# Layer 3's mixture of experts: half of each tile's weighted sum moves from VectorE to ScalarE and GpSimd, and the bias product moves behind the first experts

## What is computed

```python
router_logits = einsum('bsd,ed->bse', x, W_router) + b_router
router_weights = softmax(router_logits)       # the two largest of 8 kept, the rest set to 0
expert_out = einsum('bsd,eod->bseo', x, W_experts) + b_experts
out = einsum('bseo,bse->bso', expert_out, router_weights)
...
x = x + tanh(g_ffn[3]) * L3_ffn(layernorm(x))
```

## Time and profile before

| | us |
|---|---|
| median of 3 runs | 1064.07 (1063.49 to 1065.72) |
| the profiled execution, its own time | 1065.34 |
| its span in the profile | 1063.6 |
| PE busy | 905.5 (85%) |
| DVE busy | 709.5 (67%) |
| ACT busy | 457.7 (43%) |
| POOL busy | 104.8 (10%) |

### The profile page before, as it was taken

One profiled execution on the slowest core, in us unless ns is written; L12 is line 12 of the kernel. 1 busy time (PEld: TensorE's weight loads), 2 busy tenths in 40 slices (PEclk: granted clock), 3 DMA queues, 4 the chain that ended last, 5 costly groups with the idle time before them and its releaser, 6 DMA issues.

```text
span 1063.6 us, 14472 instructions
## 1 busy us (share of the span) xinstructions
PE 905.5 (85%) x4795; PEld 608.3 (57%) x4795; DVE 709.5 (67%) x2190; ACT 457.7 (43%) x1101; POOL 104.8 (10%) x175
## 2 busy tenths in 40 slices
PE   2459899997877878978999999999999888889967
PEld 2434544543343555665667677677667666667744
DVE  0962652639295695895848858658856787877845
ACT  0514455567767656566354263253153222212200
POOL 3100000004031130130000101000100200000000
PEclk9669999998898999999999999999999999999987
DMA  9400000000000000000000000000000000000000
GB/s 260 144 2 1 1 1 1 1 1 1 0 1 1 1 1 1 1 2 1 1 1 2 1 1 1 1 1 1 1 1 1 1 1 11 1 11 1 1 11 10
DMA packets 12066, 12.72 MB, mean 12 GB/s; under 512 B 3759, under 2 KB 7897, under 8 KB 11993
## 3 DMA queue, kind: packets, MB, share of 16 engines
q10 hardware_dynamic: 5536, 8.04, 2.5%
q1 hardware_dynamic: 6072, 3.24, 1.1%
q0 software_dynamic: 384, 0.53, 0.3%
HBM read 10.75 MB, written 1.05 MB: 11 GB/s over the span
## 4 chain that ended last, share of the span: by engine, by line
PE 57%; DVE 23%; ACT 6%; issue 5%; POOL 2%; POOLq 0%; ACTq 0%; DVEq 0%
PE bank L1608 10%; PE bank L1596 6%; PE bank L1518 5%; PE bank L1598 5%; PE bank L1597 5%; PE bank L1533 4%; PE bank L1403 4%; DVE x L1313 3%; DVE nm L1153 3%; DVE hb L1297 3%; DVE hb L1288 2%; ACT PTs L957 2%; PE bank L1573 2%; DVE x L1277 2%; PE bank L1356 2%
## 5 line engine op out<-in xcount | busy, mean ns | idle before, releaser
L994 ACT ACTIVATE hb<-bank 96x512 f32<-96x512 f32 (+1 forms) x160 | 95.0, 594 | 244.8 <-PE bank L1598 244.1
L1608 PEld LDWEIGHTS bank<-m_w,hb 128*128 128x128 f32 (+1 forms) x1280 | 165.9, 194 | 22.5 <-issue 4.9
L1596 PE MATMUL bank<-parts,m_w_lo 128*96 128x512 f32 (+1 forms) x320 | 151.9, 475 | 29.9 <-DVE hb L1288 20.5
L1608 PE MATMUL bank<-m_w,hb 128*128 128x128 f32 (+1 forms) x1280 | 175.4, 281 | 2.2 <-DVE hb L1288 2.0
L1297 DVE SCALAR_TENSOR_TENSOR hb<-hb,bank 96x512 f32<-96x512 f32 (+1 forms) x160 | 109.0, 682 | 93.8 <-ACT hb L994 93.0
L1598 PE MATMUL bank<-parts,m_w_hi 128*96 128x512 f32 (+1 forms) x320 | 127.2, 398 | 0.0
L1597 PE MATMUL bank<-parts,m_w_hi 128*96 128x512 f32 (+1 forms) x320 | 127.0, 397 | 0.0
L1288 DVE TENSOR_TENSOR hb<-hb,bank 96x512 f32<-96x512 f32 (+1 forms) x160 | 109.7, 686 | 8.6 <-PE bank L1598 3.0
L1533 PE MATMUL bank<-Qs,KT 112*77 112x512 f32 x192 | 94.5, 517 | 10.9 <-ACT PTs L957 8.8
L1596 PEld LDWEIGHTS bank<-parts,m_w_lo 128*96 128x96 f32 (+1 forms) x320 | 59.0, 184 | 78.1 <-DVE hb L1288 32.6
L1029 DVE RECIPROCAL rden<-bank 128x16 f32<-128x16 f32 x48 | 12.2, 255 | 122.3 <-PE bank L1356 122.3
(11 more groups left out here) (271 smaller groups left out, 1525.9 us busy)
## 6 DMA issues: line engine op xcount, KB each, us to landing
m_w<-in_L_ffn_w_dram ACTq DMA_DIRECT2D x2, 1024.0 KB, 11.5
nat_m<-in_L_ffn_W_dram ACTq DMA_DIRECT2D x1, 1408.0 KB, 16.8
x<-in_x_dram SPq DMA_DIRECT2D x4, 256.0 KB, 8.4
out_dram<-x SPq DMA_DIRECT2D x4, 256.0 KB, 2.0
f_out<-in_L_ffn_Wout_dram POOLq DMA_DIRECT2D x8, 64.0 KB, 7.7
m_w<-in_L_ffn_W_experts_dram ACTq DMA_DIRECT2D x1, 512.0 KB, 17.2
ctxn<-in_ctx_dram SPq DMA_DIRECT2D x4, 38.5 KB
Wq<-in_L_xattn_Wq_dram SPq DMA_DIRECT2D x2, 64.0 KB
```

Source lines behind the costliest of these rows:

```text
L994: act.activation(hb[n % 3][0:m, :], bank[UP[u, n]][0:m, :], ACT.Tanh, scale=0.5).then_inc(*chunk_act.up(u, n))
L1596: pe.matmul(dst, w_lo, x_hi, start=True, stop=False)
L1608: op = pe.matmul(bank[7][:, t * P:(t + 1) * P], hb[n % 3][0:m, t * P:(t + 1) * P], wd, start=i == 0 and t == 0, stop=ends_expert(k, n) and ...
```

## The change

Of a tile's eight experts, DVE still weighs and sums the first four, in steps with e = 0, from bank 0. ScalarE weighs the other four (e = 4, from bank 1) into an SBUF buffer `weighed[t % 2]`, which reuses room of the attention's probabilities (`PTs`), with one `activation` Copy for each expert whose scale is the gate column. GpSimd adds the four weighed blocks in pairs, one add of 128 x 256 and one of 128 x 128. DVE adds the sum into x, one tile later (`rest`). PE's bias product and DVE's add of it move from before tile 0 into step n = 2, behind the first two products. F3's body has nine steps in place of eight, so the merge with F2 shifts a little. Bank 0 is now read by DVE alone and bank 1 by ACT alone.

```diff
+    weighed = [PTs[:, 1 + i, :].rearrange("p (j d) -> p j d", d=P) for i in range(2)]
-        return {... "F3": len(tiles)}.get(k) ...
+        return {... "F3": len(tiles) + 1}.get(k) ...
 # gpsimd body
+                for n in range(steps_body(kind(u))):
+                    if kind(u) == "F3" and n % 2:
+                        t = n // 2
+                        y = weighed[t % 2]
+                        pool.wait_ge(*rows_weighed.at(u, t))
+                        pool.tensor_tensor(y[:, 0:2, :], y[:, 0:2, :], y[:, 2:4, :], ALU.add).then_inc(*rows_paired.up(u, t))
+                        pool.wait_ge(*rows_paired.at(u, t))
+                        pool.tensor_tensor(y[:, 0, :], y[:, 0, :], y[:, 1, :], ALU.add).then_inc(*rows_summed.up(u, t))
 # scalar body
+                    act.wait_ge(*logits_vector.at(u, "whole"))
+                    if b:
+                        act.wait_ge(*x_done.at(("A", u[1] - 2)))
+                    for n, (t, e) in enumerate(tiles):
+                        if e:
+                            if t >= 2:
+                                act.wait_ge(*x_done.at(u, t - 2, "rest"))
+                            act.wait_ge(*chunk_psum.at(u, n))
+                            for j in range(E3):
+                                op = act.activation(weighed[t % 2][:, j, :], bank[n % 2][:, j * P:(j + 1) * P], ACT.Copy,
+                                                    scale=gw[s][:, t, e + j:e + j + 1])
+                            op.then_inc(*rows_weighed.up(u, t))
+                        yield
+                    yield
 # vector body
-                    (the wait for the bias and the add to x, before the first step)
+                    def rest(t):
+                        dve.wait_ge(*rows_summed.at(u, t))
+                        dve.wait_ge(*x_done.at(u, t, E3 - 1))
+                        dve.tensor_tensor(x[b][:, t, :], weighed[t % 2][:, 0, :], x[b][:, t, :], ALU.add) ...
                     for n, (t, e) in enumerate(tiles):
+                        if n == 2:
+                            (x_done of tile 0, the wait for the bias and the add to x)
+                        if e == 0:
                             (the wait for the product and its four operations)
+                            if t:
+                                rest(t - 1)
                         yield
+                    rest(T - 1)
+                    yield
 # tensor body
-                    (gates_ready, free(3), the bias product, before the first step)
                     for n, (t, e) in enumerate(tiles):
+                        if n == 2:
+                            (gates_ready, free(3), the bias product)
                         ...
-                        reader[d] = (x_done, u, t, e + E3 - 1)
+                        reader[d] = (rows_weighed, u, t) if e else (x_done, u, t, E3 - 1)
```

More of the change, by code:

```diff
@@ L658, in main @@
         "gates_ready").split())
+    rows_weighed, rows_paired, rows_summed = (sig(n) for n in "rows_weighed rows_paired rows_summed".split())
     (chunk_psum, chunk_act, chunk_silu, chunk_ready, ffn_psum,
@@ L704, in steps_body @@
             return H + 1
-        return {"A3": 3, "F0": 2 * (C0 + 1), "F3": len(tiles)}.get(k) or 3 * (len(chunks[k]) + LATE)
+        return {"A3": 3, "F0": 2 * (C0 + 1), "F3": len(tiles) + 1}.get(k) or 3 * (len(chunks[k]) + LATE)
     def steps_tail(k):
@@ L837, in body @@
             def body(u):
-                for _ in range(steps_body(kind(u))):
+                for n in range(steps_body(kind(u))):
[6 more added lines that the diff above has]
+                        pool.tensor_tensor(y[:, 0, :], y[:, 0, :], y[:, 1, :], ALU.add).then_inc(*rows_summed.up(u, t))
                     yield
@@ L999, in body @@
                 if k == "F3":
-                    for _ in tiles:
+                    act.wait_ge(*logits_vector.at(u, "whole"))
[10 more added lines that the diff above has]
+                            op.then_inc(*rows_weighed.up(u, t))
                         yield
+                    yield
             def tail(u):
@@ L1303, in body @@
                 if k == "F3":
[L1304 to L1307, removed]
-                    for n, (t, e) in enumerate(tiles):
[L1309 to L1315, removed]
+                    def rest(t):
+                        dve.wait_ge(*rows_summed.at(u, t))
+                        dve.wait_ge(*x_done.at(u, t, E3 - 1))
+                        dve.tensor_tensor(x[b][:, t, :], weighed[t % 2][:, 0, :], x[b][:, t, :], ALU.add) \
+                            .then_inc(*x_done.up(*((u,) if t + 1 == T else (u, t, "rest"))))
@@ new lines, in body @@
+                    for n, (t, e) in enumerate(tiles):
+                        if n == 2:
+                            dve.wait_ge(*x_done.at(u, 0, E3 - 1))
+                            dve.wait_ge(*ffn_psum.at(u, "bias"))
+                            dve.tensor_tensor(x[b][:].rearrange("p t d -> p (t d)"), bank[3][:],
+                                              x[b][:].rearrange("p t d -> p (t d)"), ALU.add).then_inc(*x_done.up(u, "bias"))
+                            dve.wait_ge(*x_done.at(u, "bias"))
+                        if e == 0:
+                            dve.wait_ge(*chunk_psum.at(u, n))
+                            for j in range(E3):
+                                if j:
+                                    dve.wait_ge(*x_done.at(u, t, j - 1))
+                                dve.scalar_tensor_tensor(out=x[b][:, t, :], in0=bank[n % 2][:, j * P:(j + 1) * P],
+                                                         scalar=gw[s][:, t, j:j + 1], in1=x[b][:, t, :],
+                                                         op0=ALU.mult, op1=ALU.add).then_inc(*x_done.up(u, t, j))
+                            if t:
+                                rest(t - 1)
@@ L1316, in body @@
                         yield
-                    x_done.counts[(u,)] = x_done.counts[(u, T - 1, MOE3 - 1)]
+                    rest(T - 1)
+                    yield
             def tail(u):
@@ L1641, in body @@
                 if k == "F3":
[L1642 to L1647, removed]
                     pe.wait_ge(*xf_low.at(u))
                     for n, (t, e) in enumerate(tiles):
+                        if n == 2:
+                            pe.wait_ge(*gates_ready.at(u))
+                            free(3)
+                            for i in range(T):
+                                op = pe.matmul(bank[3][:, i * P:(i + 1) * P], gT[:, i * P:(i + 1) * P], m3_b[:], start=i == 0, stop=i == T - 1)
+                            op.then_inc(*ffn_psum.up(u, "bias"))
+                            reader[3] = (x_done, u, "bias")
                         d = n % 2
```

## The result

The changed kernel takes 1056.95 us (median of 4 executions, 1055.78 to 1060.12) beside 1063.78 for the kernel before on the same chip (1062.61 to 1065.72, 4 executions): a ratio of 0.9941, 95% interval 0.9914 to 0.9968, or 6.8 us less. The forecast was 1055.7 in a range of 1052.0 to 1060.5. The profiled execution took 1060.12 with a span of 1058.4, so it is 3 us above its own median, and part of the story is why. Two executions of the kernel before that stand beside its second trace ran in a slower state (1219 and 2284 us) and are left out of every number.

The account below looks back on a forecast made before the run. DVE was taken to bound F3's bodies in streams 0 to 2, and its own chain stream 3. Savings of 6.1 us (streams 0 to 2) and 2.3 (stream 3) made 8.4, giving 1055.7 us, range 1052 to 1060.5.

Parts of the forecast that it names:

- Streams 0 to 2: F3's bodies beside F2: PE becomes the bound at 94% busy, saving 2.7, 1.6 and 1.8 us, together 6.1.
- the bias product's move: F3's start: bias product (1.15 us) falls behind product 1; its DVE add (0.69) is moved, not removed.
- the ninth step: F3's merge with F2: the extra step shifts F2 by less than a step, costed at nothing, 1 us either way.
- Stream 3: Running alone at the end: store at 1058.6 against 1061.17, 2.6 us saved, taken as 2.3 (1.3 to 2.8).
- ACT: Weighing an odd product: four weighed blocks take 1.14 us, bounds 0.95 and 1.45.
- POOL: Adding the weighed blocks in pairs: 0.61 and 0.40 us, 1.08 a tile with hand-over, bounds 0.9 and 1.35.
- `rest(t - 1)`: DVE's add of the earlier tile's sum, merged part: its 2.3 us path is hidden for t = 0 to 2.
- A: F3 of streams 0 to 2: PE takes over as the bound, 7 to 11 us won; chance 0.62.
- B: F3's hand-overs: waits at `rest(3)`, for bank 0 or late F2 pairs eat half, 3 to 5 us won; chance 0.18.
- C: POOL's adds: DVE waits at every `rest`; gain gone at 2.3 us a pair, 1072 us at 2.8; chance 0.05.
- D: A3 after F3 starts earlier: more than 11 us won, 1 to 1.5 for streams 0 and 1 each; chance 0.10.
- E: F2's own chain holds PE, only stream 3 counts and the step shift cancels it: 1063 to 1065 us; chance 0.05.

Follow-up runs that it names:

- second trace: The kernel before run once more with no edit: 1064.57 us, ratio 1.0008 to itself.
- the two series of the changed kernel: The changed kernel measured first, 1056.95 us (ratio 0.9941), and again with no edit, 1058.67 us (ratio 0.9949).
- relieved kernel: Changed kernel in eight steps, with DVE doing one of its four weighed sums per tile in streams 0 to 2: 1054.01 us, ratio 0.9917.
- eight steps: The changed kernel without the ninth step, `rest(3)` standing at the end of the eighth: 1058.07 us, ratio 0.9947.
- the two others with nine steps: Changed kernel with ACT and POOL taking experts 0 to 3, DVE 4 to 7 in two banks: 1057.10 us; changed kernel with one more POOL add per tile: 1060.68.
- four eight-step ones: Changed kernel in eight steps: as such, 1058.07 us; streams 0 to 2 only, 1059.43; DVE's products in two banks, 1056.27; ACT and POOL taking experts 0 to 3, 1056.41.
- streams 0 to 2 alone: Streams 0 to 2 as changed but in eight steps, stream 3 as in the kernel before: 1059.43 us, ratio 0.9951.
- the pair at 2.09: The changed kernel with a further POOL add of 128 x 256 into an unused buffer ahead of each pair: 1060.68 us, ratio 0.9974.

## Why the prediction was right, point by point

**In short:** the mechanism was right, the time fell into the range, and the sum was too large: 8.4 us forecast, 6.8 and 5.5 in the two series of the changed kernel. That the total came as near as it did is in part luck, since an oversized term and a missing one have opposite signs.

**The bound and the direction** were right. DVE was the bound of F3's bodies, and with half of its sums gone PE is: 94% and 91% busy, windows of 16.36 and 16.60 us. The relieved kernel confirms it from the other side, with 2 to 3 us for another 13.7 of DVE's work.

**Streams 0 to 2** were forecast at 6.1 us and gave 4.5 in nine steps (5.1 to 6.0 in eight) at full clock. They are not spread as forecast: streams 0 and 1 were to win 4.3 and the stretch beside them won 5.3 to 5.8; stream 2 was to win 1.8 and its stretch lost about 1 in nine steps and won 0.1 in eight. Three terms of the sum are to be mended. First, stream 2's window was cut to the last operation on x, 1.3 us past PE's last down product, and that end counted as PE's idle time. A window of the kernel before that ends with PE's last down product:

```profile
988.00:1013.40 25.40, 23.57 (x136) 19.18 (x134) 22.37 (x55) 4.16 (x7) 0.00 (x0) 1.00 0.00 1
```

PE was busy 93% already. From the forecast's own start, 991.57, to PE's end at 1013.36 it is 20.00 of 21.79 us, 92%, and lifting that to 94% is worth 0.5, not 1.8. Second, the bias product's move was costed at nothing in these streams, and alone it wins about 1.9 us of F. Third, the ninth step costs 1 us. So mended the sum says 6.1 - 1.3 + 1.9 - 1.0 = 5.7, still 1.2 more than was measured: the relief of DVE won less than the 94% promised, or part of it is what the move had won already. No kernel here has the relief without the move, so the share of each isn't shown.

**The clock** was no term at all in streams 0 to 2. The changed kernel's traces lost 5.1 and 1.7 us to it in F, the two others with nine steps 2.0 and 3.5, the kernel before's two 0.2 and 3.4. Some low stretches come back at the same place in kernels with the same steps (near 857 to 863 in all four nine-step traces, between 933 and 939 in four eight-step ones), others don't, and not every wait of PE is followed by one. Whether the change makes them more frequent is not settled: two traces of the kernel before are too few.

**Stream 3** was walked right: 2.6 from the walk, 2.62 measured, a tile 2.57 for 2.65. Some 0.2 of it is the clock's: in "streams 0 to 2 alone", whose stream 3 is that of before, the stretch takes 15.04 at a granted clock of 1.00, where the trace before took 15.26 at 0.89; at full clock the change is worth 2.4. The cut to 2.3 for a product at low clock was unneeded: the granted clock was 1.00 in that window.

**ACT** 1.14 for four blocks, exactly (the overlap that the forecast gives as 105 ns works out at 109 from its rows). **POOL** 1.29 from the start of the first add to `rest` (1054.34 to 1055.63) where 1.08 + 0.04 was taken, inside the bound of 1.35. The row behind the price, L834 in the earlier trace rows, is a multiplication that reads one operand twice, and not an add; the adds here read two. **`rest(t - 1)`** never waits for t = 0 to 2 (2.5 us of waiting in all, in two places, 1.56 of them at the end), and the wait at `rest(3)` was 0.95 in stream 0 and none in streams 1 and 2, where up to 1 was forecast. In eight steps it is 1.15, 1.43 and 1.83.

**The rivals.** A's mechanism happened, but its gain stayed below its 7 to 11 us with 5.5 to 6.8; of its range, 1053 to 1057.5, the first series (1056.95) is inside and the second (1058.67) isn't. B gave 3 to 5, which the intervals of the two series (3.4 to 9.1 and 3.8 to 6.9 us) don't exclude. Its mechanism isn't seen in the changed kernel, where DVE stands 0.95 for `rest(3)` in one of streams 0 to 2 and not 2.3 in each; in eight steps it comes nearer, and still F is shorter there. C did not happen, since POOL's pair took 1.29 with its hand-over, under the 1.8 from which C counts. Its price was not far off: with the pair at 2.09 its rule gives 16 x 0.29 = 4.6 us of loss, and 2.7 to 3.5 were measured. D needed the following A3 to start earlier; even the relieved kernel, with 8 us in F, only reached 9 in all by its ratio. E is refuted by the kernel with streams 0 to 2 alone, which won 5 us without stream 3. The page cited with rival C, the Trainium skill's "SBUF — State Buffer", § Who interferes with whom, has the pair right: `rest`, with two SBUF inputs, slowed beside POOL's adds, and the weighed sums, with one input in PSUM, did not (0.35 either way). But `rest` took 0.17 us more where the add still ran on for 0.30 (1046.06 to 1046.36), and 0.42 more with 0.62 beside adds, so a block in full isn't what these rows show; and in the changed kernel `rest` came when POOL was done.

## What to carry to other kernels

When work is moved off an engine, look for what else moved with it, and run that part alone: here a small product and its add, moved behind the first products, let DVE's first sum start 0.7 to 1.35 us sooner and alone won about 1.9 us in the merged streams, where the whole change won 4.5. Look at the stretches one by one as well: all of the 4.5 and more came beside one feed-forward, and beside the other the kernel lost about 1. Cut a window at the end of the engine that is to become the bound, not at the end of the one being relieved. And set low-clock time aside before comparing two traces: here it differed by 3 us between two executions of one kernel, as much as the effect in question.

## What the runs showed of the hardware that was not expected

- A GpSimd add of two different f32 operands in SBUF took 461 ns for 128 columns and 730 for 256, 2.1 ns a column, where the multiplication that reads one operand twice (308 columns in 700, 4 in 199) works out at 1.65. The Trainium skill, "GPSIMD Engine Reference", § 3.1 Elementwise — side-by-side cycle accounting, has about 2.6 cycles an element for two inputs read through one port, from which 2.2 ns at the 1.2 GHz of its example is an estimate; the runs' 2.1 agrees, and the estimate would have given the slope that the nearest row didn't.
- A `tensor_tensor` add of DVE with both inputs in SBUF took 0.28 us by itself, 0.45 with 0.30 of it beside a GpSimd add, and 0.70 with 0.62 beside adds.
- The granted clock fell to 1.2 GHz's level behind a wait of PE of 2.59 us in one kernel and stayed at 2.4 behind 3.21 at the same place in another. In one and the same kernel it stayed up behind a wait of 2.26 in one execution and was low behind 2.28 in another.
